# Signals of TensorE by quads of chunks, and one GpSimd wait for every eight gathers, in a graph-network kernel

## The reference

```python
h = relu(layernorm(x))
# layer 0: two weighted means over neighbours, 128 features each
x_fwd = segment_sum(w * h[dst, :128], src) / clip(degree(src), 1)
x_bwd = segment_sum(w * h[src, 128:], dst) / clip(degree(dst), 1)
x = x + concatenate([x_fwd, x_bwd])
h = relu(layernorm(x))
# layer 1: graph attention, eight heads of 64, then one of 256
def gat(x, W, b, a, g, beta):
    h = x @ W.T + b
    score = (h @ a[:d])[src] + (h @ a[d:])[dst]
    e = exp(-leaky_relu(score, 0.2))
    return layernorm(segment_sum(e[:, None] * h[dst], src)) * g + beta
x = x + elu(gat(concatenate([elu(gat(h, head)) for head in heads]), out))
```

## Time and profile before

| what | value |
|---|---|
| median of 3 runs | 3293.55 us (3287.83 to 3297.24) |
| the profiled execution, its own time | 3294.2 us |
| its span in the trace | 3292.4 us |
| mean granted TensorE clock, share of full | 0.825 |
| TensorE busy | 2243.2 us (68%), 14916 matmuls |
| TensorE weight loads busy | 1669.3 us (51%) |
| VectorE busy | 1917.8 us (58%) |
| ScalarE busy | 1738.7 us (53%) |
| GpSimd busy | 1928.0 us (59%), of it 1820.1 in 1856 gathers |

### The profile page before, as it was taken

One profiled execution on the slowest core, in us unless ns is written; L12 is line 12 of the kernel. 1 busy time (PEld: TensorE's weight loads), 2 busy tenths in 40 slices (PEclk: granted clock), 3 DMA queues, 4 the chain that ended last, 5 costly groups with the idle time before them and its releaser, 6 DMA issues. The chain is left out here.

```text
span 3292.4 us, 46358 instructions
## 1 busy us (share of the span) xinstructions
PE 2243.2 (68%) x14916; PEld 1669.3 (51%) x14916; DVE 1917.8 (58%) x4213; ACT 1738.7 (53%) x5133; POOL 1928.0 (59%) x1999
## 2 busy tenths in 40 slices
PE   6887778677758877343577777777767566655653
PEld 4785667567747766233343333333335445444542
DVE  8985788577747776222446666666686233333336
ACT  3995677578747776222334444344438344444444
POOL 1006666666666666666635656665645566666664
PEclk8998999799878999555688888888888777777776
DMA  2011111111141112111545656665641333333335
GB/s 60 1 41 40 40 44 43 43 45 45 45 47 44 45 44 53 47 46 47 58 140 160 169 164 173 169 170 157 168 104 33 87 92 89 91 89 90 90 90 77
DMA packets 114882, 270.48 MB, mean 82 GB/s; under 512 B 34543, under 2 KB 51670, under 8 KB 114646
## 3 DMA queue, kind: packets, MB, share of 16 engines
q0 software_dynamic: 89088, 245.53, 30.5%
q1 hardware_dynamic: 25558, 21.98, 2.1%
HBM read 250.96 MB, written 16.42 MB: 81 GB/s over the span
## 5 line engine op out<-in xcount | busy, mean ns | idle before, releaser
L435 POOL DMA_INDIRECT rows_near<-table_a,s_idx_S x464 | 474.1, 1022 | 286.0 <-issue 115.4
L435 POOL DMA_INDIRECT given<-table,s_idx_S x464 | 449.2, 968 | 301.5 <-issue 126.8
L1166 DVE TENSOR_TENSOR work<-work,bank 128x129 f32 (+2 forms) x928 | 391.0, 421 | 362.4 <-remote 163.1
L435 POOL DMA_INDIRECT rows_near<-table,s_idx_S x464 | 446.8, 963 | 252.7 <-issue 127.8
L435 POOL DMA_INDIRECT rows_near<-table_b,s_idx_D x464 | 450.0, 970 | 230.9 <-issue 101.9
L950 PE MATMUL bank<-scratch,oh 128*128 128x512 f32 x928 | 488.1, 675 | 15.9 <-DVE scratch L1413 11.7
L818 PE MATMUL bank<-rows_near,oh 128*128 128x129 f32 x1856 | 331.0, 330 | 246.6 <-issue 179.5
L647 ACT ACTIVATE e_att<-lrelu 128x32 f32<-128x32 f32 (+1 forms) x232 | 49.9, 215 | 740.6 <-DVE lrelu L1402 490.0
L818 PEld LDWEIGHTS bank<-rows_near,oh 128*128 128x128 f32 x1856 | 289.0, 234 | 282.1 <-issue 232.8
L935 PE MATMUL bank<-sort_ring,scratch 128*128 x2784 | 154.0, 169 | 329.4 <-ACT scratch L643 285.2
L538 ACT ACTIVATE scratch<-scratch,given 128x128 f16<-128x128 bf16 x840 | 284.1, 388 | 170.8 <-DVE scratch L1130 146.7
(11 more groups left out here) (222 smaller groups left out, 4799.8 us busy)
## 6 DMA issues: line engine op xcount, KB each, us to landing
rows_near<-table_a,s_idx_S POOLq DMA_INDIRECT x464
rows_near<-table_b,s_idx_D POOLq DMA_INDIRECT x464
rows_near<-table,s_idx_S POOLq DMA_INDIRECT x464
given<-table,s_idx_S POOLq DMA_INDIRECT x464
table<-scratch SPq DMA_DIRECT2D x25, 260.0 KB
table<-scratch SPq DMA_DIRECT2D x25, 128.5 KB, 3.0
xs<-in_x SPq DMA_DIRECT2D x1, 3072.0 KB
out_x<-scratch SPq DMA_DIRECT2D x24, 128.0 KB, 1.7
```

Source lines behind the costliest of these rows:

```text
L435: nc.gpsimd.indirect_dma_start(out=to, out_offset=None, in_=table[:, :], in_offset=bass.IndirectOffsetOnAxis(ap=s_idx[order][:, c:c + 1], ...
L1166: v.tensor_add(a, a, psum).then_inc(sum_free[o], 1)
```

## The change

TensorE signals once for each quad. In layer 0 `chunks_summed`, one increment a chunk, becomes `quads_summed`, one a quad. In the attentions the signals of the turned quad (`ohT_psum`) and of the source scores (`ssrc_ready`) become one, `turned_and_scored`, fired by the last transpose of quad q+2, which TensorE issues behind the source scores of quad q+1; `sum_ready` fires once a quad instead of once a group. ScalarE's copy, VectorE's scores and its group sums wait on the new counts. GpSimd waits only before every eighth gather, and there for all eight slots that the next eight gathers fill. No other instruction is added or removed. The diff, cut to its core (the declarations are left out):

```diff
                 for c in range(CHUNKS):
                     if c in CUT:
                         pool.wait_ge(edges_sorted, phase * 2 + CUT.index(c) + 1)
-                    pool.wait_ge(chunks_summed, phase * CHUNKS + c + 1)
+                    if c % (2 * QUAD) == 0:
+                        pool.wait_ge(quads_summed, phase * QUADS + c // QUAD + 2)
                     gather(table, rows0[:, c % SLOTS, 0:HALF], order, c)
 
             def gather_layer1(o, table, width):
                 for c in range(CHUNKS):
-                    if c >= SLOTS and o == "1":
-                        pool.wait_ge(msg_ready[o], c + 1 - SLOTS)
-                    elif c >= SLOTS:
-                        pool.wait_ge(sum_ready[o], (c - SLOTS) // GP + 1)
+                    if c >= SLOTS and c % (2 * QUAD) == 0 and o == "1":
+                        pool.wait_ge(msg_ready[o], c + 2 * QUAD - SLOTS)
+                    elif c >= SLOTS and c % (2 * QUAD) == 0:
+                        pool.wait_ge(sum_ready[o], (c - SLOTS) // QUAD + 2)
                     gather(table, row_slots(c % SLOTS, 1)[:, 0, 0:width], "S", c)
 
 
...
                                          scale=-1.0, bias=ones[:, 0:1]).then_inc(oh_ready[o], 1)
 
                 def transposed(q, u):
-                    act.wait_ge(ohT_psum[o], q + 1)
+                    if isinstance(q, int) and q < 2:
+                        act.wait_ge(turned_and_scored[o], q + 1)
+                    else:
+                        act.wait_ge(turned_and_scored[o], q + 2)
                     nc.scalar.activation(ohT[:, u % 2, :], turned[u % 2], ACT.Copy).then_inc(ohT_ready[o], 1)
 
                 def weights(q, u):
...
                             transposed(i * UNROLL + (u + 2), u)
                         if not isinstance(i, int) or q + 3 < QUADS:
                             if not isinstance(i, int) or q >= 1:
-                                act.wait_ge(sum_ready[o], i * (2 * UNROLL) + 2 * u)
+                                act.wait_ge(sum_ready[o], i * UNROLL + u)
                             one_hots(i * UNROLL + (u + 3), u + 3)
                         if o == "1":
                             beside_heads(q)
...
                     if k == 0:
                         pe.wait_ge(sum_free[o], g + QUAD // GP)
                     pe.wait_ge(rows_scaled, phase * CHUNKS + c + 1)
-                    nc.tensor.matmul(sum0(g), oh[:, slot, :], rows0[:, slot, :],
-                                     start=(k % GP == 0), stop=(k % GP == GP - 1)).then_inc(chunks_summed, 1)
+                    last = nc.tensor.matmul(sum0(g), oh[:, slot, :], rows0[:, slot, :],
+                                            start=(k % GP == 0), stop=(k % GP == GP - 1))
+                last.then_inc(quads_summed, 1)
 
             for t in range(T):
                 if t == 2:
...
                     for k in range(QUAD):
                         upper = oh[:, u % UNROLL * QUAD + k, :].bitcast(BF16)[:, 1:2 * P:2]
                         last = nc.tensor.transpose(turned[u % 2][:, k * P:(k + 1) * P], upper, ident_bf[:, :])
-                    last.then_inc(ohT_psum[o], 1)
+                    return last
 
                 def source_scores(q, u, tiles):
 
...
                             last = nc.tensor.matmul(bank[2 + u % 2][:, k * heads:(k + 1) * heads], ohT[:, u % 2, k * P:(k + 1) * P],
                                                     s_parts[:, f, bass.ds(tiles[k // 2], 1), 0:heads].rearrange("p t h -> p (t h)"),
                                                     start=(f == 0), stop=(f == 2))
-                    last.then_inc(ssrc_ready[o], 1)
+                    return last
 
                 def sums(q, u):
                     for k in range(QUAD):
...
                             lanes, rows = oh[:, u * QUAD + k, :], m
                         else:
                             lanes, rows = m[:, 0:P], row_slots(u * QUAD + k, 1)[:, 0, 0:width]
-                        mm = nc.tensor.matmul(bank[4 + u % 2 * 2 + k // GP][:, 0:width], lanes, rows,
-                                              start=(k % GP == 0), stop=(k % GP == GP - 1))
-                        if k % GP == GP - 1:
-                            mm.then_inc(sum_ready[o], 1)
+                        last = nc.tensor.matmul(bank[4 + u % 2 * 2 + k // GP][:, 0:width], lanes, rows,
+                                                start=(k % GP == 0), stop=(k % GP == GP - 1))
+                    last.then_inc(sum_ready[o], 1)
 
                 def turn(i):
                     n = 2 * UNROLL if not isinstance(i, int) or i < ROUNDS - 1 else 2 * UNROLL - 2
...
                     for u in range(UNROLL):
                         q = i * UNROLL + u
                         if not isinstance(i, int) or q + 1 < QUADS:
-                            source_scores(i * UNROLL + (u + 1), u + 1, tiles[2 * u:2 * u + 2])
-                        if not isinstance(i, int) or q + 2 < QUADS:
-                            transposed(i * UNROLL + (u + 2), u + 2)
+                            last = source_scores(i * UNROLL + (u + 1), u + 1, tiles[2 * u:2 * u + 2])
+                            if not isinstance(i, int) or q + 2 < QUADS:
+                                last = transposed(i * UNROLL + (u + 2), u + 2)
+                            last.then_inc(turned_and_scored[o], 1)
                         sums(q, u)
 
-                transposed(0, 0)
-                transposed(1, 1)
-                source_scores(0, 0, tile_numbers(mybir.EngineType.PE, "S", TILE_AT, 2))
+                transposed(0, 0).then_inc(turned_and_scored[o], 1)
+                transposed(1, 1).then_inc(turned_and_scored[o], 1)
+                source_scores(0, 0, tile_numbers(mybir.EngineType.PE, "S", TILE_AT, 2)).then_inc(turned_and_scored[o], 1)
                 turn(0)
                 for i in range(1, ROUNDS - 1):
                     turn(i)
...
             v.tensor_scalar(unsplit[0:32, :], ident[0:32, 0:T], 256.0, None, ALU.mult)
             link(v.tensor_copy(unsplit[32:64, :], ident[32:64, 32:32 + T]))
             dve.sem_inc(consts_made, 1)
-            dve.sem_inc(chunks_summed, SLOTS)
+            dve.sem_inc(quads_summed, SLOTS // QUAD)
             dve.sem_inc(col_free, RING)
             for o in "SD":
                 dve.sem_inc(sum_free[o], SUMS0)
...
 
             def one_hots(o, phase, q):
 
-                dve.wait_ge(chunks_summed, phase * CHUNKS + q * QUAD + QUAD)
+                dve.wait_ge(quads_summed, phase * QUADS + q + 1)
                 v.tensor_tensor(oh[:, q * QUAD % SLOTS:q * QUAD % SLOTS + QUAD, :],
                                 (iota_f[:, 0:P] if phase and q >= FIRST else iota_sum).unsqueeze(1).to_broadcast([P, QUAD, P]),
                                 s_lo[o][:, q * QUAD:(q + 1) * QUAD].unsqueeze(2).to_broadcast([P, QUAD, P]),
...
 
             def add_sums(o, phase, q, tiles):
 
-                dve.wait_ge(chunks_summed, SLOTS + phase * CHUNKS + QUAD * (q + 1))
+                dve.wait_ge(quads_summed, SLOTS // QUAD + phase * QUADS + q + 1)
                 for j in range(2):
                     g = q * 2 + j
                     add_group(o, acc[o], tiles[j], g, sum0(g), SUMS0)
...
                 def scores(i, q, u):
 
                     n = QUAD * heads
-                    dve.wait_ge(ssrc_ready[o], q + 1)
+                    dve.wait_ge(turned_and_scored[o], q + 3)
                     for k in range(QUAD):
                         b = u % UNROLL * QUAD + k
                         dve.wait_ge(gathered[b], i * 16 + 16 * ((1 + int(o)) * ROUNDS + 1 + u // UNROLL))
...
                         ins.then_inc(msg_ready[o], 1)
 
                 def add_groups(q, u, tiles):
+                    dve.wait_ge(sum_ready[o], q + 1)
                     for j in range(2):
-                        dve.wait_ge(sum_ready[o], q * 2 + (j + 1))
                         add_group(o, acc, tiles[j], q * 2 + j, bank[4 + u % 2 * 2 + j][:, 0:width], 4)
 
                 def turn(i):
```

More of the change, by code:

```diff
@@ L313, in build @@
         gathered = [sem(f"gathered{i}") for i in range(SLOTS)]
-        chunks_summed = sem("chunks_summed")
+        quads_summed = sem("quads_summed")
         oh_ready = {o: sem(f"oh_ready_{o}") for o in "SD12"}
@@ L317, in build @@
         sum_free = {o: sem(f"sum_free_{o}") for o in "SD12"}
-        ohT_psum = {o: sem(f"ohT_psum_{o}") for o in "12"}
+        turned_and_scored = {o: sem(f"turned_and_scored_{o}") for o in "12"}
         ohT_ready = {o: sem(f"ohT_ready_{o}") for o in "12"}
-        ssrc_ready = {o: sem(f"ssrc_ready_{o}") for o in "12"}
         off_made = {o: sem(f"off_made_{o}") for o in "12"}
```

## The result

The changed kernel takes **3452.51 us** (median of 4, 3416.09 to 3465.51) against 3290.69 before (median of 4): a ratio of 1.0477, 95% interval 1.0440 to 1.0513. It is slower; the forecast was 3342.5 with a range up to 3440.

A forecast was written before the change was run, and what follows sets the result against it. GpSimd's gathers and pauses bound it, TensorE's signals coming late behind queued matmuls. Terms -22, +33, +38 and 0 gave +49: 3343.2 us profiled, 3342.5 as median; own range 3308 to 3385, with rivals 3190 to 3440.

The forecast's parts named there:

- Signals removed: 0: TensorE's signals cut from 1856 to 700 gain nothing, since no matmul is removed.
- merged signal: 0: Attentions: VectorE's scores wait for four more transposes, covered in the first attention by 0.9 us of its messages; 0.
- The rival of the merged signal: Attentions: source scores' signal sits behind four more matmuls, 1.41 us more per VectorE stall, +122; 3427 in all; chance 0.15.
- Second attention: 0: GpSimd already pauses at every eighth gather, so waits fall on the same places; 0, bounds -29 and +82.
- First attention: +38: GpSimd waits three messages more, 1.9 us, in 20 of 30 long pauses; +38, bounds 0 and +124.
- Late layer 0: -22: 1330 to 1645: gathers stream at 1.25 us, 0.5 us pause per eight, 293 against 315; bounds -36 and 0.
- The rest of layer 0: +33: 256 to 1330: coarse waits see signals up to 1.1 us later in 89 groups; a third taken, bounds 0 and +98.
- Its signs: Expected if right: late layer 0 about 293 us, first attention about 780 with pauses near 7, VectorE's "remote" waits about unchanged.
- the rival that the signals are the queue: GpSimd's waits in layer 0: fewer signals pass unhindered, -120 us, 3174 in all; chance 0.22.
- the pauses become useful: One coarse pause lets everything through: rest of layer 0 -44, attentions hold, 3258 in all; chance 0.13.

The follow-up runs named there:

- e4: The kernel before with each quad's twelve source-score matmuls done twice, no more signals: 3366.69 us, ratio 1.0227.
- e6: The kernel before with three more wide matmuls (448 columns) a quad into a part nobody reads: 3355.00 us, ratio 1.0070.
- e1: TensorE's half of the change alone (signals by quads, merged signal), GpSimd waiting before every gather as in the kernel before: 3300.09 us, ratio 1.0028.
- e3: The kernel before with 7592 more TensorE signals on semaphores nobody reads: 3315.45 us, ratio 1.0071.
- e2: The kernel before with only GpSimd's waits of the change, at every eighth gather for eight slots: 3433.38 us, ratio 1.0431.
- e11: The changed kernel with three memsets as a stop in every eight gathers of the first attention: 3362.07 us, ratio 1.0094 to the kernel before.
- e13: The kernel before with three memsets as a stop in every eight gathers of the first attention: 3275.96 us, ratio 0.9846.
- e16: The kernel before with two memsets as a stop in every eight gathers of the first attention: 3328.01 us, ratio 1.0001.

## Why the prediction was wrong

What bounds the kernel was read rightly: GpSimd's pauses, made by TensorE's signals that come late while gathers stream and all come in a pause; and what is queued goes more by matmuls (e4, e6) than by signals (e1, e3). The forecast's sign, the place and the part at fault were those of its terms; the sizes were not.

- **Signals removed: 0, merged signal: 0.** Right in the main; e1 holds both and measures +9 us. The rival of the merged signal had the nearest number, 3427, for the wrong reason.
- **Second attention: 0.** Right: 680 us in both profiles.
- **First attention: +38.** It measured +81 in the profiles. This is the step that failed. The 1.9 us for the later message were right (1.7 in the rows), but it was multiplied by 20 on the ground that "the gathers after it no longer stop and the queue is empty". It is the other way about: gathers that don't stop fill the queue again. Sixteen run at a stretch, the short pauses that let signals through are gone, and each round then waits through the whole chain from signal to message: 234 us of such waits instead of 152. There are 28 rounds with a wait and not 20; at 1.7 us each the later message is an estimated 48 of the 81, and the other 33 are pauses that grew longer.
- **Late layer 0: -22.** Measured +7 (223 gathers from 319 to 326 us by GpSimd's timeline). The gathers did stream at 1.25 us; the assumed stop of 0.5 us in each group of eight was in truth one of 4.3 us in each twenty-four, of up to 13.0 at the longest. e2, with the same waits, has no pause above 5.2 us there and takes 318 us.
- **The rest of layer 0: +33.** Measured +36 in the first sum and +10 in the early part of the second, 46: within its bounds, a third too low. The bounds of the attention, 0 to +124, held as well; what was wrong was to take the low third of each. The dense layer between the attentions, 122 us before and 114 after, gave 8 back.
- **The range.** The profiled execution lies inside it, the median does not. The bounds of the forecast's own terms add up to -65 and +304, so to 3229 and 3598 us, yet its own range was put at 3308 to 3385, with no reason given for so narrow a one; 3452.5 lies within those bounds. Also, the terms were made for one execution of each, and the changed kernel's executions spread over 49 us where the kernel before had 11. Nothing in the forecast allowed for that.
- **Its signs.** The long pause near 7 us at every second group of eight came (6.73 and 6.83 us). Late layer 0 took 327 us and not 293, the attention 824 and not 780, and the "remote" waits of VectorE's scores grew, from 179.1 us to 244.2 in the first attention and from 303.5 to 328.3 in the second.
- **Readings that don't hold.** Of the 57.3 us that GpSimd waits for the sort in the first sum, 53.3 lie before the first gather (at 255.5 us) and so outside the pauses; the rival that the signals are the queue would have had some 160 us to gain by its own sum and not 120. And the 247 of 962 to 1330 counts six instructions that are no gathers.

The rival "the pauses become useful" rested on the right mechanism and had it backwards: coarse waits make fewer pauses, not better ones. The Trainium skill, "NOTIFIC — the notification-queue block", section "7.1 Overflow: three behaviours, one of which stalls the engine", speaks of an internal pipeline that pushes back. That would go with a queue of matmuls; no run here shows that it is that block. Every execution timed here, and not only the profiled ones, is on record with a span and a granted clock, so each was recorded while it ran: whether the signals would be late without the recording no run tells.

## What to carry to other kernels

Where one engine issues gathers back to back and another's signals come late, don't count only what a wait costs but also what its pauses let through: here fewer and coarser waits cost 4.3%, and a deliberate stop of 2 us in every eight gathers of one stage gained 1.5%. When a row shows that a stall is ended by the stall itself, ask of a change whether it makes stalls rarer and longer. And test a suspected queue by what fills it: the same busy time as few large instructions and as many small ones.

## What the runs showed of the hardware

- While GpSimd issues gathers at a pitch of 1.25 us, TensorE's signals are seen up to 8.5 us late; in the long pauses shown they are seen 2.4 to 3.3 us after the last gather has begun (e11 2.4, the changed kernel 3.1, before 3.3), whether GpSimd idles or does a memset.
- A stop with 2.92 us from gather to gather lets them through (46 of 56 in e11, 47 of 56 in e13), one with 2.34 us mostly doesn't (21 of 56 in e16).
- What the lateness costs goes, in all, with the number of TensorE's matmuls more than with its time: twelve small ones more a quad cost 75 us, three large ones 23; 7592 signals more cost 24 us.
- Which part of the chip is shared by gathers and TensorE's signals no run here tells.
